# Attention over 1601 keys: the odd 64 keys of two heads in one tile, and key 1600 as side work

## The reference, cut to what matters

```python
q, k, v = query @ wq + bq, key @ wk + bk, value @ wv + bv      # 16 heads of 16
score = einsum('bhqd,bhkd->bhqk', q, k) / sqrt(16) + (1.0 - mask) * -1e9
alpha = softmax(score, axis=-1)
x = x + einsum('bhqk,bhkd->bhqd', alpha, v).reshape(b, -1, 256) @ wo + bo
```

## Time and profile before

| | us |
|---|---|
| median of 3 runs | 1293.83 (1291.77 to 1296.13) |
| the profiled execution | 1307.28, its span 1305.5 |
| PE busy | 1178.0 (90%) |
| ACT busy | 1038.3 (80%) |
| DVE busy | 677.9 (52%) |
| POOL busy | 174.1 (13%) |

### The profile page before, as it was taken

How to read it: one execution, slowest core, us unless ns; L and a number is a source line. 1 busy time by engine, 2 the same in 40 slices (tenths; PEclk the granted TensorE clock), 3 DMA queues, 4 the chain that set the end, 5 groups by cost and what they waited for, 6 DMA issues and landing times. The chain is left out here.

```text
span 1305.5 us, 43625 instructions
## 1 busy us (share of the span) xinstructions
PE 1178.0 (90%) x17942; PEld 583.4 (45%) x17942; DVE 677.9 (52%) x1622; ACT 1038.3 (80%) x1482; POOL 174.1 (13%) x211
## 2 busy tenths in 40 slices
PE   8888798898898999999999999977879999998995
PEld 5322232232222356677899988642222223222222
DVE  5325656756646576554666666653235343333335
ACT  3599899999999855443666666539999999999993
POOL 5111111011001030333000010323120000000000
PEclk9999999999999999999999999989999999999997
DMA  6236734534636333211443354222120010010001
GB/s 189 67 115 228 249 105 138 177 105 147 194 108 219 92 116 108 91 64 49 121 139 106 113 153 126 81 71 81 38 60 11 19 29 2 19 28 2 3 3 65
DMA packets 106305, 124.94 MB, mean 96 GB/s; under 512 B 25091, under 2 KB 89310, under 8 KB 106142
## 3 DMA queue, kind: packets, MB, share of 16 engines
q1 hardware_dynamic: 89088, 85.95, 21.5%
q0 software_dynamic: 9328, 29.37, 7.2%
q10 hardware_dynamic: 7726, 7.26, 1.9%
HBM read 70.27 MB, written 46.95 MB: 90 GB/s over the span
## 5 line engine op out<-in xcount | busy, mean ns | idle before, releaser
L888 ACT ACTIVATE prob<-banks 128x1024 f32<-128x1024 f32 (+1 forms) x832 | 772.5, 1048 | 17.8 <-PE banks L1679 14.1
L1694 PE MATMUL banks<-prob,v 64*32 64x512 f32 x6656 | 443.7, 594 | 0.6 <-ACT prob L888 0.6
L1679 PE MATMUL banks<-zone,kst 52*32 52x512 f16 x6528 | 336.7, 384 | 90.4 <-ACT prob L888 82.5
L1679 PEld LDWEIGHTS banks<-zone,kst 52*32 52x32 f16 x6528 | 92.7, 89 | 500.3 <-ACT prob L888 478.4
L1694 PEld LDWEIGHTS banks<-prob,v 64*32 64x32 f32 x6656 | 119.1, 106 | 22.0 <-ACT prob L888 2.4
L2327 PE MATMUL banks<-xsT_d,w 128*128 128x128 f16 x1776 | 123.6, 219 | 3.3 <-DMA w<-weight_parts 1.5
L2327 PEld LDWEIGHTS banks<-xsT_d,w 128*128 128x128 f16 x1776 | 108.7, 98 | 12.3 <-issue 9.2
L2338 PE MATMUL banks<-w,hh 128*128 128x256 f16 x592 | 107.0, 273 | 0.0
L2124 DVE TENSOR_TENSOR hl<-hid,hh 128x128 f16<-128x128 f32 x296 | 83.3, 291 | 31.8 <-ACT hh L2051 23.7
L2047 ACT ACTIVATE hid<-banks,b 128x128 f32<-128x128 f32 x222 | 74.5, 368 | 25.1 <-PE banks L2327 21.0
L2290 PE MATMUL banks<-w,hh 128*128 128x256 f16 x480 | 80.6, 276 | 2.0 <-DVE outb_d L2209 2.0
(11 more groups left out here) (275 smaller groups left out, 1289.0 us busy)
## 6 DMA issues: line engine op xcount, KB each, us to landing
weight_parts<-late SPq DMA_DIRECT2D x54, 256.0 KB, 3.4
w<-weight_parts POOLq DMA_DIRECT2D x24, 512.0 KB, 4.0
late<-in_L_ffn_W_r SPq DMA_DIRECT2D x43, 256.0 KB, 4.2
weight_parts<-more SPq DMA_DIRECT2D x26, 256.0 KB, 3.3
zone<-q_parts SPq DMA_DIRECT2D x180, 32.0 KB
slot_rows<-late POOLq DMA_DIRECT2D x14, 384.0 KB, 4.4
more<-in_L_ffn_W_r SPq DMA_DIRECT2D x21, 256.0 KB, 4.1
xs_d<-slot_rows ACTq DMA_DIRECT2D x39, 128.0 KB, 2.1
```

The source lines that it names most:

```text
L888: nc.scalar.activation(prob[0:m, t % P_RING, 2 * (n % 2):2 * (n % 2) + 2, :], score[G % S_RING][0:m, :, :], ACT.Exp, scale=0.25).then_inc( ...
L1679: last = nc.tensor.matmul(score[G % S_RING][j:j + wide, a, :], kst[stack, 2 * q + n % 2, t * P + j:t * P + j + wide], qst[stack, u % Q_RIN ...
L1694: last = nc.tensor.matmul(outp[u % 2][GROUP * j:GROUP * (j + 1), a, :], v[rows, t, u % NQ, j, :], prob[rows, (u * KT + t) % P_RING, j, :], ...
```

## The change

- PAIRS becomes 25. Tiles 0 to 11 stay. Of the last tile only 64 keys stay, and all four heads share one score group: `packed_half` says in which half of the rows a head's keys stand. One exponential of 128x1024 takes the place of two of 65x1024. `outputs` of that tile has four products instead of eight.
- Key 1600 becomes a side piece "last" in tile LAST_AT = 2 of every unit. `last_scores` computes its score for four heads, each repeated over 32 rows. DVE transposes it in blocks of 32 (`take_last`, behind `finish`, in unit 0 behind `claim_late`). ACT takes a 128x16 exponential of it, for unit u - 1 behind the first exponential of unit u, and for the last unit behind the loop. At the head of `finish` DVE spreads it with another block transpose (`spread_last`), and a multiply-add with the key's value takes the place of the copy L1170.
- The key's values come from `project_last_value`, 32 products with one moving column on PE, in layer 0 ahead of the bounds, in layer 1 ahead of the first values, and from `last_values`, four small instructions on DVE.
- The other side pieces move to other tiles, mostly one tile later, and `side_pieces` gets a new order.
- POOL's three memsets for the upper half of the last value tile fall away.

```diff
-PAIRS = 2 * KT
+PAIRS = 2 * (KT - 1) + 1
+PACKED = PAIRS - 1
...
-SIDES_AT = [((6, 7, 9, 10), (2, 3, 5, 6, 8, 9), (2, 4, 6, 8), (2, 4, 6)),
-            ((2, 4, 6, 7, 9, 10), (2, 4, 5, 7, 9, 10), (2, 4, 6, 8, 10, 11), (2, 4, 5, 7, 8, 10))]
-LATE_AT = ((), (7, 9), (2, 4, 6, 8), ())
+LAST_AT = 2
+SIDES_AT = [((6, 7, 9, 10), (3, 4, 6, 7, 9, 10), (3, 5, 7, 9), (4, 6, 8)),
+            ((3, 5, 7, 8, 10, 11), (3, 5, 6, 8, 10, 11), (3, 5, 7, 8, 10, 11), (3, 5, 6, 8, 9, 11))]
+LATE_AT = ((), (7, 9), (3, 5, 7, 9), ())
...
+        lasts = [[("last", c, q)] if c < NC else [] for q in range(NQ)]
+        waves = [("wave", c - 1, i) for i in range(TPC)] if done else []
         if layer == 0:
-            order += outs + turns + asked[:1] + back + asked[1:] + ([("logit", c - 1, 0)] if done else [])
+            order += lasts[0] + outs[:1] + lasts[1] + outs[1:] + turns + lasts[2] + asked[:1] + back
+            order += lasts[3] + asked[1:] + ([("logit", c - 1, 0)] if done else [])
+        elif c == 0:
+            order += lasts[0] + lasts[1] + turns + lasts[2] + asked + lasts[3]
         else:
-            order += turns + outs if c >= 1 else outs + turns
-            order += asked + back + ([("wave", c - 1, i) for i in range(TPC)] if done else [])
+            order += lasts[0] + turns + outs[:1] + lasts[1] + outs[1:] + asked[:1]
+            order += lasts[2] + asked[1:] + back + waves[:1] + lasts[3] + waves[1:]
     return {name: n for n, name in enumerate(order)}
 
...
+                    "logit": NQ * (c + 1) + 3, "wave": NQ * (c + 1) + 2 + min(i, 1), "last": NQ * c + i}[name]
+
+        def packed_half(j):
+
+            return j % 2 if j < 2 else 1 - j % 2
+
+        def last_tile(a, j):
+
+            return KT - 1 if a == packed_half(j) else KT - 2
+
+        def exps_before(u, t):
+            return PAIRS * u + 2 * t
 
...
-                nc.gpsimd.memset(v[HALF:P, KT - 1], 0.0).then_inc(v_cleared, 1)
-                for b in range(2):
-                    pool.wait_ge(v_cleared, 3 + b)
-                    nc.gpsimd.memset(beside(b)[HALF:KLAST, KT - 1:KT], 1.0).then_inc(v_cleared, 1)
-                pool.wait_ge(v_cleared, 5)
...
+            def last_exponentials(u):
+
+                act.wait_ge(side_free, at["last", u // NQ, u % NQ] + 1)
+                nc.scalar.activation(lastexp[:], osum.rearrange("p (n r) -> p n r", r=GROUP)[:, :, 0], ACT.Exp, scale=0.25).then_inc(last_exp, 1)
+
             act.wait_ge(v_ready, KT)
             for u in range(UNITS):
                 for n in range(PAIRS):
-                    G, t, m = u * PAIRS + n, u * KT + n // 2, m_of(n // 2)
+                    G, t = u * PAIRS + n, u * KT + n // 2
                     act.wait_ge(scores_done, G + 1)
                     if n % 2 == 0 and t >= P_RING:
                         act.wait_ge(pv_done, t - P_RING + 1)
-                    nc.scalar.activation(prob[0:m, t % P_RING, 2 * (n % 2):2 * (n % 2) + 2, :],
-                                         score[G % S_RING][0:m, :, :], ACT.Exp, scale=0.25).then_inc(exp_done, 1)
+                    nc.scalar.activation(prob[:, t % P_RING, 2 * (n % 2):2 * (n % 2) + 2, :],
+                                         score[G % S_RING], ACT.Exp, scale=0.25).then_inc(exp_done, 1)
+                    if u and n == 0:
+                        last_exponentials(u - 1)
+            last_exponentials(UNITS - 1)
             if first:
...
+            def last_values():
+                dve.wait_ge(last_projected, 1)
+                if first:
+                    dve.wait_ge(prepared, 4)
+                for i in range(DH):
+                    for b in range(2):
+                        nc.vector.scalar_tensor_tensor(vlast[:, i, b:b + 1], lastp[:, i, b:b + 1], g.lanes[:, b:b + 1], g.lanes[:, 1 - b:2 - b],
+                                                       ALU.mult, ALU.add).then_inc(last_ready, 1)
...
+                for i, (_, o, n) in enumerate(bounds):
                     bound_product(o, n)
+                    if i == 2:
+                        last_values()
                     if n == len(BCH) - 1:
...
+                last_values()
...
+            def take_last(u):
+                bank = take("last", u // NQ, u % NQ)
+                nc.vector.transpose(osum, bank).then_inc(side_free, 1)
+
+            def spread_last(u):
+
+                dve.wait_ge(last_exp, u + 1)
+                nc.vector.transpose(osum, lastexp[:].unsqueeze(2).broadcast_to([P, CH // GROUP, GROUP])).then_inc(last_spread, 1)
+                dve.wait_ge(last_spread, u + 1)
+
             def finish(u):
 
                 c, q = u // NQ, u % NQ
                 i, b = q // 2, q % 2
+                spread_last(u)
                 dve.wait_ge(pv_done, KT * (u + 1))
-                nc.vector.tensor_copy(osum, outp[u % 2][:, 0, :]).then_inc(half_read, 1)
+                nc.vector.scalar_tensor_tensor(osum, osum, vlast[:, i, b:b + 1], outp[u % 2][:, 0, :],
+                                               ALU.mult, ALU.add).then_inc(half_read, 1)
                 dve.wait_ge(half_read, u + 1)
                 nc.vector.tensor_tensor(osum, osum, outp[u % 2][:, 1, :], ALU.add).then_inc(out_read, 1)
...
                 if u:
                     finish(u - 1)
+                    take_last(u)
...
                         normalise(c + 1)
                         claim_late()
+                        take_last(0)
                     cuts(u, 0, 1)
...
+                    if t < KT - 1:
+                        last = nc.tensor.matmul(project[t % 2][:, 0:D], g.ctxT[:, h, t * P:(t + 1) * P], wv[:, h, :],
+                                                start=(h == 0), stop=(h == DH - 1))
+                    else:
+                        for a in range(2):
+                            last = nc.tensor.matmul(project[t % 2][HALF * a:HALF * (a + 1), 0:D], g.ctxT[:, h, t * P:t * P + HALF], wv[:, h, :],
+                                                    start=(h == 0), stop=(h == DH - 1), tile_position=(0, HALF * a))
                 last.then_inc(v_projected, 1)
+
+            def project_last_value():
+                for i in range(DH):
+                    for b in range(2):
+                        for j in range(QH):
+                            n0 = i * P + b * HALF + (j - b) * HD
+                            for c in range(DH):
+                                last = nc.tensor.matmul(lastp[GROUP * j:GROUP * (j + 1), i, b:b + 1], wv[:, c, n0:n0 + GROUP],
+                                                        g.ctxT[:, c, KV - 1:KV], start=(c == 0), stop=(c == DH - 1),
+                                                        tile_position=(0, GROUP * j))
+                last.then_inc(last_projected, 1)
...
+                project_last_value()
...
+                project_last_value()
...
                 u, n = G // PAIRS, G % PAIRS
-                q, t, m = u % NQ, n // 2, m_of(n // 2)
+                q, t = u % NQ, n // 2
                 if G >= S_RING:
                     pe.wait_ge(exp_done, G - S_RING + 1)
                 if n == 0:
                     pe.wait_ge(q_loaded[u % Q_RING], 16 * loads_of(u))
                     if u < NQ:
                         pe.wait_ge(k_loaded[q], 16 * K_LOADS)
-                for j in range(0, m, GROUP):
-                    wide = min(GROUP, m - j)
-                    for a in range(2):
-                        stack = slice(HALF * a, HALF * a + STACK)
-                        last = nc.tensor.matmul(score[G % S_RING][j:j + wide, a, :], kst[stack, 2 * q + n % 2, t * P + j:t * P + j + wide],
-                                                qst[stack, u % Q_RING, n % 2, :], start=True, stop=True,
-                                                tile_position=(HALF * a, j))
+                if n < PACKED:
+                    for j in range(0, P, GROUP):
+                        for a in range(2):
+                            stack = slice(HALF * a, HALF * a + STACK)
+                            last = nc.tensor.matmul(score[G % S_RING][j:j + GROUP, a, :], kst[stack, 2 * q + n % 2, t * P + j:t * P + j + GROUP],
+                                                    qst[stack, u % Q_RING, n % 2, :], start=True, stop=True,
+                                                    tile_position=(HALF * a, j))
+                else:
+                    for k in range(0, HALF, GROUP):
+                        for j in range(QH):
+                            a, i = j % 2, j // 2
+                            stack, row = slice(HALF * a, HALF * a + STACK), HALF * packed_half(j) + k
+                            last = nc.tensor.matmul(score[G % S_RING][row:row + GROUP, i, :], kst[stack, 2 * q + i, t * P + k:t * P + k + GROUP],
+                                                    qst[stack, u % Q_RING, i, :], start=True, stop=True,
+                                                    tile_position=(HALF * a, row))
                 last.then_inc(scores_done, 1)
+
```

(24 more changed lines are left out.)

## The result

The changed kernel takes 1318.23 us, median of 3 runs (1311.85 to 1320.47). Against the kernel before that is a ratio of 1.0168, 95% interval 1.014 to 1.0197: 1.7% slower. The forecast was 1306 in a range from 1294 to 1319. The direction is right and the time lies at the upper edge of the range; the median moved by 24.4 us where the sum said 12.2.

The account below looks back on a forecast made before the run. ACT's exponentials were taken to set the pace in both attentions. The terms -20.7 + 4.5 + 8.5 + 6.2 + 5.4 + 4 + 3 + 1 + 0.3 gave +12.2 us on the median 1293.8: 1306, range 1294 to 1319.

Parts of the forecast that it names:

- The saving: ACT, 30 units: one exponential fewer, less the small one and a PE charge, 0.69 us a unit, -20.7 us (-9 to -27).
- PE becomes the bound: Rival, every unit: PE has little slack, each unit loses 0.4 us instead of 0.07; 1316 us, chance 0.12.
- ACT behind `take_last(0)`: Unit 1, both layers: ACT's exponentials wait in order until DVE transposes after the key loads; +4.5 and +8.5 us.
- The piece at tile 2: Layer 0, units 2 and 3: PE waits for DVE's late `finish`; +6.2 us, and 9.7 lost against 4.3 before (+5.4).
- Restarts: PE after waits: lower granted clock and a second ACT gap, three more such restarts; +3 us (1 to 7).
- Late reads elsewhere: Unit 4 and two or three later units: `finish` reads late for the moved pieces; +4 us (0 to 9).
- The base: Kernel before: unit 3 of layer 0 already lost 4.3 us; the summed difference was put on the median, 1293.8 us.
- The end: End of each layer: the last spreading transpose runs beside the last values; +0.3 us (0 to 1.4).
- The start of layer 1: PE's `project_last_value`, 64 matmuls taken as 3.5 us, mostly covered by the wait for POOL's memsets; +1 us (-1 to 4).
- longer restarts and more late reads: Rival: 7 us for restarts instead of 3 and 9 for late reads instead of 4; 1315 us, chance 0.10.
- the lateness would be absorbed: Rival, layer 0: cuts' loads land sooner, so reads of units 2 to 4 precede tile 2; 1288 us, chance 0.11.
- halve: Rival: only half the losses at tile 2, and 1.5 us for restarts; +2.9 us, 1297 us, chance 0.15.

Follow-up runs that it names:

- small_twice: Changed kernel with unit 0's transpose earlier, unit 1's key-1600 piece later and DVE cuts earlier; ACT takes each small exponential twice: 1278.8 us, ratio 0.9871.
- packing_alone: Changed kernel without key 1600's scores, transposes, small exponential and multiply-add; packed tile and moved pieces stay: 1269.9 us, ratio 0.9803.
- early_take: Changed kernel with only unit 0's key-1600 score transposed into xpT's memory, ahead of the wait for key loads: 1306.48 us, ratio 1.009.
- fewer_ahead: Changed kernel with unit 0's transpose earlier, key-1600 pieces later in early units, and layer 0's DVE cuts earlier (three in unit 1): 1272.89 us, ratio 0.9824.

## Why the direction was right, and where the sizes were wrong

- **The saving** of 0.69 us a quiet unit (-20.7): 0.75 in layer 0, and 0.46 to 0.83, on average 0.67, in units 5 to 13 of layer 1. In layer 0 that is a step of 0.90 less 0.12 for the small exponential and some 0.03. In layer 1 the terms are others, and that their mean is near the forecast is luck: the small exponential costs these nine units nothing (small_twice, packing_alone), and what makes them fall short of a step of 0.90, by 0.23 on average, is PE in the tiles with side pieces and at the heads of units. They fall short by as much in packing_alone, so it isn't the work for key 1600; whether it is the packed tile or the moved pieces, no run separates. The rival "PE becomes the bound" holds in these places, with 0.23 a unit where it had 0.4. The quiet units were to take 22.9 to 23.5 us: units 5 to 7 of layer 0 take 23.2 to 23.6, those of layer 1 up to 24.4.
- **The small exponential**: taken 0.15, and it holds ACT 0.12 to 0.13 (926.95 to 927.08 in the changed kernel, 1031.16 to 1031.28 in small_twice).
- **ACT behind `take_last(0)`**: +4.5 and +8.5 forecast; ACT stood 5.12 and 8.67 us, and early_take shows that moving the transpose ahead ends both stops. ACT did not pass the waiting exponential in either layer, as the Trainium skill, "TensorE: Matmul & The Clock Gate", section "Architectural detail: the array is 16× 32×32, not 1× 128×128", has it of its queue; here the two stops are 13.8 us.
- **The piece at tile 2**: +6.2 and 9.7 forecast for units 2 and 3; PE stood 5.75 and 9.04 us there, and the units were 7.5 and 10.8 us over the 23.3 that they take without the wait. The reads ended at 118.9 and 153.0, forecast 116.3 and 149.0.
- **Restarts**: forecast +3, the term most mis-sized with the next. ACT's later gaps behind a stop are 1.06 and 0.62 (unit 1), 1.11 and 0.43 (units 2 and 3), 1.11 and 0.62 (unit 12), 1.11 (unit 14) and 1.05 (layer 1, unit 1): 8.7 us behind six stops, where I had counted three.
- **Late reads elsewhere**: forecast +4. Over what the units take in fewer_ahead, unit 4 lost 1.2, unit 8 0.5, unit 12 5.3, unit 14 3.0 and unit 3 of layer 1 1.9: 11.9 us with their restarts, 10 in the second execution. ACT at units 12 and 14:

```profile
371.86 1.02 ACT L910 ACTIVATE prob<-banks 128x1024 f32<-128x1024 f32 x1 [3.28 <-PE banks L1750]
...
422.34 1.02 ACT L910 ACTIVATE prob<-banks 128x1024 f32<-128x1024 f32 x1 [1.45 <-PE banks L1750]
```

- **The base**: I credited the 4.3 us that unit 3 lost before. That execution was 12 us longer than the runs; in a second one the unit lost 1.3. I had put the whole difference on the median instead of asking which of its waits the other runs don't have.
- **The end**: +0.3 forecast; from the last exponential on the span is 1.8 us longer (33.7 and 31.9), and as much in packing_alone, so it is not the spreading transpose. No run tells what it is.
- **The start of layer 1**: +1 forecast for `project_last_value`, from 3.5 on PE. Its 64 products took 0.81 us in layer 0 and 1.24 in layer 1, and there they ended at 865.84, while the first values waited for POOL until 868.47. Nothing was lost by them:

```profile
864.60 1.24 PE L1647 MATMUL banks<-ctxT,pre 128*32 128x1 f32 x64
...
868.47 0.79 ACT L847 ACTIVATE v<-banks 128x128 f32<-128x128 f32 x4 [1.46 <-POOL v L657]
```

So the losses, each over what the unit takes in fewer_ahead, are 7.1 + 10.1 (unit 1 of both layers) + 7.5 + 10.8 + 11.9 = 47.4 us with their restarts, where the forecast had 4.5 + 8.5 + 6.2 + 9.7 + 4 + 3 = 35.9. These 11.5 us are about what the sum was short of. The rest nearly cancels: the base is 3.0 and the end 1.5 more than forecast, the saving over all 32 units 2.2 us better (22.9 in fewer_ahead against the second execution of before, unit 3's wait left out), and the 1 us at the start of layer 1 didn't come. The mechanism of the losses was the forecast's; the sizes were those of the rival "longer restarts and more late reads", 7 and 9, to which I had given 0.10. That the lateness would be absorbed, or halve, is refuted: units 2 and 3 lost the same in both executions.

## What to carry to other kernels

A saving on the bound engine came out near its cost, on average; the cost of new side work was in its places, not in its instructions. When a small step is put into an engine's order, look for the latest of what it waits for and for all that stands behind it, and move the step, or the work that makes its release late, before giving up the saving. A late release that nobody waits for costs nothing, until the first consumer is placed in front of it. A stop of PE can cost more than its own length: the stops of 3.4 to 9.6 us here were all followed by a restart of 0.9 us or more, those of 1.3 to 2.7 us in some executions only.

## What the runs showed of the hardware

After a stop of PE of 5.75 us the granted clock was 0.50 for some 5 us, and ACT lost 1.5 us more there; behind stops of ACT of 3.3 us and of 9.0 us the later gaps were the same, 1.1 and 0.4 to 0.6 us. A stop of the same length need not end alike: after PE's 1.54 us in unit 14 the clock was 0.50 in one execution and 1.00 in the other, and the same holds for its 2.23 us in unit 3 of layer 1, where the unit took 26.3 and 24.9. The 128x16 exponential lasts 0.22 to 0.34 us and holds the next one back only 0.12 to 0.13. And a word in the trace, "issue", stood for a wait on a semaphore that came 0.1 us before the instruction began.
